# Second adder layer of a fused network kernel: pair sums by accumulating DMA, key table on GpSimd

## The reference

```python
def adder2d(x, w, stride=1, padding=0):
    """out[n,co,ho,wo] = -sum_{ci,kh,kw} |x_patch - w[co,ci,kh,kw]|."""
    ...
out = conv2d(x, w_shift1)                       # 1x1
out = adder2d(out, w_add1)                      # 1x1
out = relu(batchnorm(out, ...))
out = conv2d(out, w_shift2, padding=1)          # 3x3
out = adder2d(out, w_add2, padding=1)           # 3x3: the second adder layer
out = relu(batchnorm(out, ...))
return relu(out + identity)
...
def step(h, p):                                 # scanned over 33 sets of weights
    op = argmax(h[0, 0, :19])
    y = attention(h, p[...][op]); h = where(p['am'][op], y, h)
    z = relu(h @ w1[op] + b1[op]) @ w2[op] + b2[op]
    h = where(p['fm'][op], z, h)
```

## Time and profile before

| | us |
|---|---|
| median of 3 runs (369.09 to 369.84) | 369.75 |
| the profiled execution | 370.56 |
| its span, first to last instruction | 368.8 |
| second adder layer's groups on PE | 42.94 to 138.76 |

### The profile page before, as it was taken

One profiled execution on the slowest core, in us unless ns is written; L12 is line 12 of the kernel. 1 busy time (PEld: TensorE's weight loads), 2 busy tenths in 40 slices (PEclk: granted clock), 3 DMA queues, 4 the chain that ended last, 5 costly groups with the idle time before them and its releaser, 6 DMA issues.

```text
span 368.8 us, 11416 instructions
## 1 busy us (share of the span) xinstructions
PE 349.0 (95%) x5069; PEld 214.6 (58%) x5069; DVE 221.7 (60%) x329; ACT 177.0 (48%) x174; POOL 19.9 (5%) x40
## 2 busy tenths in 40 slices
PE   8899999999999998899999998778999999999996
PEld 6535547753333335764653344454677777788884
DVE  1779999999999996674937775265411111111112
ACT  2871897878887952144837776213111111111111
POOL 3481000000000002000000000000000000000000
PEclk9999999999999999999989999899999999999999
DMA  5718200000000006300000000000140000000001
GB/s 169 221 21 277 77 2 2 2 2 2 3 2 2 2 0 235 129 5 17 1 2 2 4 0 2 6 0 0 34 102 4 4 4 4 2 4 4 4 4 45
DMA packets 10192, 12.86 MB, mean 35 GB/s; under 512 B 4102, under 2 KB 8984, under 8 KB 10136
## 3 DMA queue, kind: packets, MB, share of 16 engines
q1 hardware_dynamic: 9160, 8.85, 7.9%
q0 software_dynamic: 832, 3.00, 2.5%
q10 hardware_dynamic: 144, 0.20, 0.2%
HBM read 10.44 MB, written 0.40 MB: 29 GB/s over the span
## 4 chain that ended last, share of the span: by engine, by line
PE 82%; DVE 5%; issue 3%; ACT 2%; DMA 2%; SPq 1%; DVEq 0%; ACTq 0%
PE PS L930 82%; DVE RSC L543 1%; DMA W1R<-in_fwa 1%; DMA W4R<-in_aw 1%; DVE pool_ L872 1%; DVE TMP L732 1%; DVE pool_ L760 1%; DVE pool_ L584 1%; ACT pool_ L455 0%; ACT SDC L347 0%; ACT H1P L378 0%; DVE X L775 0%; DVE TMP L773 0%; SPq L256 0%; ACT VT L437 0%
## 5 line engine op out<-in xcount | busy, mean ns | idle before, releaser
L930 PE MATMUL PS<-pool_,CON 128*32 128x392 f32 (+2 forms) x1320 | 110.2, 493 | 0.6 <-DVE pool_ L760 0.4
L405 ACT ACTIVATE pool_<-TMP,WA 128x3136 f32<-128x3136 f32 x27 | 78.1, 2927 | 12.2 <-PE PS L930 11.4
L930 PEld LDWEIGHTS PS<-pool_,CON 128*32 128x32 f32 (+1 forms) x1320 | 49.5, 110 | 59.2 <-issue 46.4
L760 DVE TENSOR_SCALAR pool_<-TMP,WA 128x3136 f32<-128x3136 f32 x45 | 81.4, 1852 | 0.2
L918 DVE COPY pool_<-PS 128x392 f32<-128x392 f32 x32 | 18.1, 567 | 82.5 <-PE PS L930 82.5
L503 ACT ACTIVATE pool_<-PS 128x392 f32<-128x392 f32 x32 | 15.9, 497 | 83.3 <-PE PS L930 83.3
L930 PE MATMUL PS<-pool_,WS 128*32 128x392 f32 (+3 forms) x1024 | 46.6, 333 | 0.0
L930 PE MATMUL PS<-HE,WS 128*32 128x392 f32 (+3 forms) x1024 | 46.5, 333 | 0.1
L930 PEld LDWEIGHTS PS<-pool_,WS 128*32 128x32 f32 x1024 | 36.4, 110 | 10.6 <-issue 2.7
L930 PEld LDWEIGHTS PS<-HE,WS 128*32 128x32 f32 x1024 | 36.0, 111 | 11.2 <-issue 3.0
L930 PE MATMUL PS<-CON 128*128 128x196 f32 (+1 forms) x202 | 39.0, 338 | 1.0 <-DVE QZ L576 0.5
(11 more groups left out here) (222 smaller groups left out, 299.5 us busy)
## 6 DMA issues: line engine op xcount, KB each, us to landing
pool_<-in_pho SPq DMA_DIRECT2D x1, 3144.0 KB, 11.9
HE<-in_phe SPq DMA_DIRECT2D x1, 3136.0 KB, 11.9
QZ<-CW SPq DMA_DIRECT2D x12, 98.0 KB, 2.3
CW<-in_cw POOLq DMA_DIRECT2D x2, 576.0 KB, 4.7
CON<-in_con POOLq DMA_DIRECT2D x1, 732.5 KB, 6.0
out_y<-Y SPq DMA_DIRECT2D x1, 392.0 KB, 2.4
CQ<-in_ws SPq DMA_DIRECT2D x16, 9.0 KB
MPP<-in_mpp POOLq DMA_DIRECT2D x1, 256.0 KB, 3.0
```

What stands on the lines that cost most here:

```text
L405: a.activation(RING[:, g % RG, :, :].rearrange("p b (r c) -> p b r c", r=SIDE), window(n // CQ), ACT.Abs, bias=WA2[:, n:n + 1], scale=-1.0 ...
L760: v.tensor_scalar(RING[:, g % RG, :, :].rearrange("p b (r c) -> p b r c", r=SIDE), window(n // CQ), WA2[:, n:n + 1], None, ALU.max).then_i ...
L930: return t.matmul(out_, lhsT, rhs, start=start, stop=stop, skip_group_check=True)
```

## The change

Eight of DVE's 45 units, those with n % 8 == 2 in the taps 0 to 7, no longer go to the ring. `PAIRED` maps them to four pairs: n = 2 and 10, 18 and 26, 34 and 42, 50 and 58. DVE writes both of a pair in succession at the first one's n, into the halves `TWO[:, 0]` and `TWO[:, 1]` of the space of `HE`. POOL issues a transfer within SBUF that adds the second half to the first (`accum_op=ALU.add`). PE reads the sum once, after its group of n = 15, 31, 47 and 63. There is one such double buffer: from the second pair on DVE waits for `pair_free`, which PE raises after a sum. `SLOT` renumbers the units that are left for the ring. The load of `HE` is issued after the sequential steps. The key table is made on POOL in seven steps after its third transfer and `xs9_ready`. Ahead of the layer PE runs 9 constant matmuls of 196 columns and 33 of one column in place of 11.

```diff
-WARM = dict(..., copies=11, ...)
+WARM = dict(..., copies=9, ...)
+SHORT = 33
...
+PAIRS, PC8, PLATE = 4, 2, 14
+PAIRED = {CQ + CQ * tap + PC8: tap // 2 for tap in range(2 * PAIRS)}
+SLOT = {g: i for i, g in enumerate(g for g in range(NG) if g not in PAIRED)}
...
         HE = sb("HE", [P, NK, NPH])
+        TWO = HE[:, :, :].rearrange("p k t -> p (k t)").rearrange("p (n b t) -> p n b t", n=2, b=NIMG)
...
-            sp.dma_start(HE[:, :, :], ...).then_inc(s["strip_in"], 16)
             sp.wait_ge(s["adder_done"], 2)
             sp.dma_start(HO[:, :, :], ...).then_inc(s["strip_in"], 16)
...
             active_steps(sp, code, step)
 
+            sp.dma_start(HE[:, :, :], ...).then_inc(s["strip_in"], 16)
             sp.wait_ge(s["u_plain"], 1)
...
+            def keys():
...
+                g.wait_ge(s["mask_in"], 32)
+                g.wait_ge(s["xs9_ready"], 1)
+                kl(g.tensor_copy(AMF[0:1, :], AMT[0:1, :]))
+                kl(g.tensor_copy(KEYT[0:1, :], FMT[0:1, :]))
+                kl(g.tensor_scalar(KEYT[0:1, :], KEYT[0:1, :], 2.0, None, ALU.mult))
+                kl(g.tensor_tensor(KEYT[0:1, :], KEYT[0:1, :], AMF[0:1, :], ALU.add))
+                kl(g.tensor_scalar(AMF[0:1, :], KEYT[0:1, :], 0.0, None, ALU.is_gt))
+                kl(g.tensor_tensor(af, af, b4, ALU.mult))
+                g.tensor_tensor(kt, kt, af, ALU.add).then_inc(s["key_ready"], 1)
...
+            for p in range(PAIRS):
+                g.wait_ge(s["pair_unit"], 2 * p + 2)
+                g.dma_start(TWO[:, 0, ...], TWO[:, 1, ...],
+                            accum_op=ALU.add, max_dma_last_dim=6272).then_inc(s["pair_sum"], 16)
+                if p == 2:
+                    keys()
...
             for n in range(9 * CQ):
...
-                if n == 66:
-                    v.tensor_copy(AMF[0:1, :], AMT[0:1, :])
-                if n == 68:
-                    kl(v.tensor_copy(KEYT[0:1, :], FMT[0:1, :]))
...
-                if not ON_ACT[g]:
-                    v.wait_ge(s["ring_free"], g - RG + 1)
-                    v.tensor_scalar(RING[:, g % RG, ...], window(n // CQ), WA2[:, n:n + 1], None, ALU.max)...
+                if g in PAIRED and n % (2 * CQ) == PC8:
+                    p = PAIRED[g]
+                    if p:
+                        v.wait_ge(s["pair_free"], p)
+                    for i in range(2):
+                        v.tensor_scalar(TWO[:, i, ...], window(n // CQ + i), WA2[:, n + CQ * i:...],
+                                        None, ALU.max).then_inc(s["pair_unit"], 1)
+                elif not ON_ACT[g] and g not in PAIRED:
+                    v.wait_ge(s["ring_free"], SLOT[g] - RG + 1)
+                    v.tensor_scalar(RING[:, SLOT[g] % RG, ...], ...).then_inc(s["dve_unit"], 1)
-            kl(v.scalar_tensor_tensor(KEYT[0:1, :], KEYT[0:1, :], 2.0, AMF[0:1, :], ALU.mult, ALU.add))
-            kl(v.tensor_scalar(AMF[0:1, :], KEYT[0:1, :], 0.0, None, ALU.is_gt))
-            kl(v.tensor_tensor(af, af, b4, ALU.mult))
-            v.tensor_tensor(kt, kt, af, ALU.add).then_inc(s["key_ready"], 1)
...
+            def pair(p):
+                t.wait_ge(s["pair_sum"], 16 * p + 16)
+                for h in range(2):
+                    for b in range(NIMG):
+                        last = mm(PS[32 * b:32 * b + 32, 6 + h, 0:HT], SEL[False][:, PC8, :], half(TWO[:, 0, b, :], h), False, False)
+                last.then_inc(s["pair_free"], 1)
...
             keep_warm(WARM["copies"], b=7)
+            for _ in range(SHORT):
+                mm(PS[0:1, 5, 500:501], CON[:, 0:1], CON[:, 0:1])
...
-                group(CQ + n, n == 0)
+                if CQ + n not in PAIRED:
+                    group(CQ + n, n == 0)
+                if n % (2 * CQ) == PC8 + PLATE - 1 and n // (2 * CQ) < PAIRS:
+                    pair(n // (2 * CQ))
```

More of the change, by code:

```diff
@@ L32 @@
 STEPS = (4, 8)
-WARM = dict(inputs=6, means=4, squares=2, deviations=4, choice=8, weights=8, exponentials=2, sums=2, copies=11, evictions=3, shifts=4, relus=4, values=1, projections=2)
+WARM = dict(inputs=6, means=4, squares=2, deviations=4, choice=8, weights=8, exponentials=2, sums=2, copies=9, evictions=3, shifts=4, relus=4, values=1, projections=2)
+SHORT = 33
 OPW = 1024
@@ L68 @@
 ON_ACT = [on_scalar(g % CQ) for g in range(NG)]
-ACT_UPTO = [sum(ON_ACT[:g]) for g in range(NG + 1)]
-DVE_UPTO = [g - a for g, a in enumerate(ACT_UPTO)]
+PAIRS, PC8, PLATE = 4, 2, 14
+PAIRED = {CQ + CQ * tap + PC8: tap // 2 for tap in range(2 * PAIRS)}
+SLOT = {g: i for i, g in enumerate(g for g in range(NG) if g not in PAIRED)}
+ACT_UPTO = {g: sum(ON_ACT[x] for x in SLOT if x <= g) for g in SLOT}
+DVE_UPTO = {g: SLOT[g] + 1 - a for g, a in ACT_UPTO.items()}
 def active_steps(e, code, step):
@@ L283, in _ @@
             active_steps(sp, code, step)
+            sp.dma_start(HE[:, :, :], bass.AP(phe.tensor, 0, [[1, P], [LE, NK], [1, NPH]])).then_inc(s["strip_in"], 16)
             sp.wait_ge(s["u_plain"], 1)
@@ L295, in _, with kl @@
         def _(g):
+            nk = 0
+            def kl(ins):
+                nonlocal nk
+                nk += 1
+                ins.then_inc(s["key_chain"], 1)
+                g.wait_ge(s["key_chain"], nk)
+            def keys():
+                af = AMF[0:1, :].rearrange("p (o b) -> p o b", o=NOPS)
+                kt = KEYT[0:1, :].rearrange("p (o b) -> p o b", o=NOPS)
+                b4 = con_("blk4", NB, 1).unsqueeze(1).to_broadcast([1, NOPS, NB])
+                g.wait_ge(s["mask_in"], 32)
[7 more added lines that the diff above has]
+                g.tensor_tensor(kt, kt, af, ALU.add).then_inc(s["key_ready"], 1)
             hd = CC["head"]
@@ L403, in _ @@
                 if ON_ACT[g]:
[L404 to L405 removed]
+                    a.wait_ge(s["ring_free"], SLOT[g] - RG + 1)
+                    a.activation(RING[:, SLOT[g] % RG, :, :].rearrange("p b (r c) -> p b r c", r=SIDE), window(n // CQ), ACT.Abs,
                                  bias=WA2[:, n:n + 1], scale=-1.0).then_inc(s["act_unit"], 1)
@@ L984, in group @@
             def group(g, fresh=False):
-                t.wait_ge(s["dve_unit"], DVE_UPTO[g + 1])
-                t.wait_ge(s["act_unit"], ACT_UPTO[g + 1])
+                if DVE_UPTO[g]:
+                    t.wait_ge(s["dve_unit"], DVE_UPTO[g])
+                if ACT_UPTO[g]:
+                    t.wait_ge(s["act_unit"], ACT_UPTO[g])
                 for h in range(2):
                     for b in range(NIMG):
-                        last = mm(PS[32 * b:32 * b + 32, 6 + h, 0:HT], SEL[ON_ACT[g]][:, g % CQ, :], half(RING[:, g % RG, b, :], h), fresh, False)
+                        last = mm(PS[32 * b:32 * b + 32, 6 + h, 0:HT], SEL[ON_ACT[g]][:, g % CQ, :], half(RING[:, SLOT[g] % RG, b, :], h), fresh, False)
                 last.then_inc(s["ring_free"], 1)
+            def pair(p):
[4 more added lines that the diff above has]
+                last.then_inc(s["pair_free"], 1)
             t.wait_ge(s["con_in"], 16)
```

18 lines of the change are left out of this document (6 added, 12 removed).

## The result

| | before | after |
|---|---|---|
| median, us | 369.69 (369.09 to 369.84, 4 runs) | 384.94 (383.89 to 385.78, 4 runs) |
| ratio, with its 95% interval | | 1.041 (1.039 to 1.044) |
| span of the profiled execution | 368.8 | 383.0 |
| first group of the layer on PE | 42.94 | 43.56 |
| the layer, to its last group's end | 95.82 | 110.86 |

The change makes the kernel slower by 15.2 us; 12.5 were forecast. In the profile it is 14.2: 0.6 before the layer, 15.0 in it, and 1.5 less behind it. The page of after, its parts on busy time and on the chain, answers to the earlier trace rows; two of its costliest groups and one of its DMA issues follow, the last to be held against the earlier trace rows.

The account below looks back on a forecast made before the run. PE was taken as the bound by a few per cent, with DVE right behind. Order 7.3, key table 3.5 and clock 1.7 sum to 12.5 us on the median of 369.75: 382.3 us, range 376 to 391 for 8 in 10.

Parts of the forecast that it names:

- Order: Second adder layer: making pairs early delays DVE's later units and PE waits; +7.3 us, the 5.3 saved already taken off.
- The three pauses: PE idles 2.9 us before n=19, 35 and 51, waiting for DVE; net +1.6 us each, +4.7 for three.
- Key table on GpSimd: Seven GpSimd steps beside DVE's units from n=50 on hold DVE up; +3.5 us taken, from 0.3 to 5.2.
- the discount below the upper end: Key table on GpSimd: 3.5 us taken, near but under the upper end of 5.2, the steps' whole time.
- Clock: PE's pauses in the layer drop its clock to half speed for 3.4 us; 0 to 3.4 us lost, +1.7 taken.
- The time after the loop: What follows the layer's loop stays as before; a change there was a named sign of being wrong.
- Sums: Transfers adding pairs within SBUF take 8 to 17 us, 14 taken, hidden since some 18 us are free.
- The rival of the late sum: Sums take above 18 us, PE waits at n=15, 31, 47 and 63, DVE behind it; 389.6 us, chance 0.18.
- Edits at nothing: One-column matmuls ahead of the layer, the later load of HE and POOL's four issues cost nothing.
- Removed work: PE works 68 groups in the layer, 5.3 us less; at most 4.1 could show, DVE standing right behind.
- the rival "faster": PE's backlog covers DVE's debt after a pair, given earlier reads or two buffers; 365.7 us, chance 0.05.
- the floor: Without any wait DVE would need 92.3 us for the layer's loop, and would then bound it.

Follow-up runs that it names:

- x1: The changed kernel with the key table back on DVE (casts at n=66 and 68, four steps behind the loop): 379.72 us, ratio 1.030.
- x5: The changed kernel with seven constant matmuls on PE ahead of n=19, 35 and 51, to fill its pauses: 385.13 us, ratio 1.043.
- x6: The changed kernel with 11 constant matmuls and no one-column ones ahead of the layer: 387.14 us, ratio 1.050.
- x9: x1 with seven constant matmuls on PE ahead of n=19, 35 and 51: 378.62 us, ratio 1.028.
- x2: x1 with PE reading each sum earlier, after n=11, 27, 43 and 59: 370.99 us, ratio 1.004.
- x12: The changed kernel with the key table still on GpSimd, begun once PE has read n=56, behind all four transfers: 380.64 us, ratio 1.031.
- x4: The kernel before with only the key table moved to GpSimd, released by xs9_ready: 376.50 us, ratio 1.020.
- x3: The changed kernel without the four transfers; PE reads both halves of each pair, 72 groups: 390.89 us, ratio 1.057.
- x8: The changed kernel with three pairs, each unit at its own n, read after n=21, 45, 69; key table on DVE, 11 copies: 371.20 us, ratio 1.005.
- x10: One pair (48, 56), units at own places, read after n=66, quantising steps and conversions later, key table on DVE, 11 constant matmuls: 377.22 us, ratio 1.021.
- x7: The kernel before with only the load of HE moved behind the sequential steps: 368.90 us, ratio 1.001.

## Why the prediction was right

It forecast 382.3 us, 376 to 391, slower; it is 384.94. Going by its own steps:

- **Order, +7.3.** Right in mechanism and in sum; two of its terms were off and cancelled. The three pauses were to be 2.9 us and are 2.89, 2.87 and, in x1 without GpSimd, 2.88; n=3 came at 48.28 (48.2 forecast); n=56 lost 0.72 in x1 (0.7). In x1 the layer ends 10.25 us later than before. Its two stretches at half clock cost 1.7 (11.12 us against 9.42 for 112 records) and 1.4 (17.42 against 16.01 for 192), which leaves 7.15. Term by term, in x1: n=3 0.9 (1.3 forecast), three pauses 5.3 (4.7; the overlap of 0.2 each was left out), n=56 0.9 (0.7), and n=24 nothing (0.6): PE at half clock came there no sooner than DVE's unit. x5, x6 and x9, at full clock there, have a wait of 0.35. x2 shows that it is the order: one number moved gives 8.7 us back, 3.1 of them the clock's.
- **Key table on GpSimd, taken +3.5 of 0.3 to 5.2.** The mechanism was right and the term too small: 5.0 us in the stretch from the pair to n=56, 4.9 in the layer, 5.2 by the medians of after and x1 (4.1 by their ratios). The step that failed is the discount below the upper end. The five steps that fall there are 3 x 1.13 + 2 x 0.59 = 4.6 us by the prediction's own prices, so DVE lost about their whole time, and nothing that can be seen slipped into gaps. "Up to 1.8 us each" was wrong as well: a step lasts 1.9 to 3.3 us here and up to 4.3 in x12. A step seems to wait for a unit, with its own work on top. The Trainium skill (SBUF — State Buffer, Who interferes with whom) says that whichever of the two comes first holds the shared ports for its whole instruction and blocks the other; these rows agree. The 5.7 us that the prediction gave by that rule was nearer than the 3.5 taken. In x4, where no step falls into a wait of DVE's, the price was 6.05 us in the layer and 7.3 in the median.
- **Clock, taken +1.7 of 0 to 3.4.** In the layer it is 3.1 that count, behind the first two pauses (2.6 by x9, since at full clock the wait at n=24 comes back). Behind the third the clock fell too, but PE was waiting for DVE there in any case, as the prediction had it. The time after the loop was taken as unchanged, and a change of it was named as a sign of being wrong. That sign came: it is 1.5 us shorter, because the stretch at half clock that before has from 188.2 to 191.6 isn't in after, while that of 236.0 to 239.4 is there at 249.7. The net is 1.6, near the 1.7 taken, but by luck: x5, whose pauses were filled, has two such stretches behind the layer, and x6, with after's pauses, 10.2 us of them.
- **Sums, taken 14 us of 8 to 17, hidden.** 11.9 us from issue to landing, landing at 58.67, 81.90 and 106.93; PE reads them at 64.36, 89.52 and 113.78. The rival of the late sum (389.6) is out, and x3 shows the transfers free of cost. It was close in one place: the fourth was issued only behind the key table, landed at 141.83 and was read at 142.45. In x8 and x10, where one issue took 7.07 and 6.70 us, a sum took 17.3 and 16.5 us from issue to landing and PE did wait for it, 1.15 and 1.39 us; that is at the forecast's upper bound of 17.
- **Edits at nothing.** Right as a whole. The one-column matmuls take 0.05 us each (33 and nine copies make 5.0 us), not 0.12, so PE's first group started 0.6 us later, not 2.8, and waited 1.89 us for n=3. The sum is the same, since DVE sets n=3. The load of `HE` is free (x7). POOL's issues last 1.77 us beside units, and DVE's units beside them are not longer (four in 7.30 us).
- **Removed work, at most 4.1.** It never showed as a gain, and the rival "faster" is out as it stood. x8, with no burst of two units, meets its condition, x2, with sums read earlier, meets it at n=19 and 35, and they still end at 371.2 and 371.0, not at 365.7. The step that fails is the floor: it took the average of DVE's work, while each place with a side job has a balance of its own.

Together: 7.15 for the order, 4.9 for GpSimd, 3.1 for the clock and 0.5 by which after begins the layer later than x1 make the 15.66 us by which the layer ends later; less 1.5 behind it, 14.2. Of the 1.7 us by which this exceeds the forecast of 12.5, the key table's term is 1.4; the medians, 15.2 us apart, add 1.0 that one profiled execution does not show.

## What to carry to other kernels

Where two engines run in step, as here, work taken off one of them is worth nothing unless the other is ahead at that place; check the balance of each stretch, not that of the loop. Units made early, two in a row, hold up all that stands behind them in the maker's order each time their buffer comes free late: ask first how many units lie between the buffer's release and the next unit that the reader wants. And a side job on GpSimd beside DVE's long units was paid by DVE about in full here, so put it where DVE waits or is ahead.

## What the runs showed of the hardware

- **GpSimd beside DVE.** Steps of one partition and 627 elements lasted 1.4 to 4.3 us beside 128x3136 fp32 units of 1.78 us, and the units 2.0 to 3.1. I had expected the steps to find gaps, as the short copies of before did in part.
- **Issuing a transfer from GpSimd.** It took 1.77 us beside the units in most cases, 0.83 and 0.84 in the fourth issue of x5 and x6, 2.44 in that of x1, x2, x9 and x12, and twice much more: 7.07 (x8) and 6.70 (x10). Both made a sum late. What sets these two apart no run tells.
- **An accumulating transfer within SBUF.** 1568 KB landed 11.9 us after its issue in after, as long as a load of 3136 KB from HBM, and delayed neither DVE nor PE (x3 without it has the same pauses to 0.03 us).
- **The clock.** It fell to 0.50 for 3.4 us behind pauses of 2.89, 2.87 and 4.56 us in after, but not behind a pause of 2.88 in x1 (120.3 to 127.0 at 1.00), nor behind one of 2.87 in x12; in x5 one came behind a pause of 2.25. In x5 and x12 it was at half from about 42.7 to 46.0 with no pause ahead, only the matmuls on constants and the eight of the x term. Behind the layer the time at half clock is 6.8 us in before, x1, x2, x5 and x9 (in one stretch in x2 and x9, in two in the others), 3.4 in after and 10.2 in x6 and x12. No run here tells what decides it.
